# Feed-forward of a decoder layer: another order inside the slots, peaks taken tile by tile, a last tile that goes round GpSimd, and final scaling on VectorE

## What is computed

```
def _act_quant(x):
    scale = 127.0 / jnp.clip(jnp.max(jnp.abs(x), axis=-1, keepdims=True), 1e-05)
    return jnp.clip(jnp.round(x * scale), -128.0, 127.0) / scale
def _bitlinear(x, w):                       # _weight_quant: three values, one scale per matrix
    return einsum('bsi,oi->bso', _act_quant(x), _weight_quant(w))
x = _layernorm(x + xattn(x, ctx))
gate = silu(_bitlinear(x, w_gate))
up = _bitlinear(x, w_up)
x = _layernorm(x + _bitlinear(gate * up, w_down))
```

## Time and profile before

| what | us |
|---|---|
| median of three runs (lowest, highest) | 812.57 (811.95, 816.28) |
| the profiled execution, its own time | 812.0 |
| span of its trace | 809.3 |
| first product of the feed-forward (L1827) starts | 673.18 |
| last product (tile 31) starts | 789.78 |
| from there to the end of the span | 19.5 |
| busy: PE, DVE, ACT, POOL | 697.6, 638.6, 380.4, 376.9 |

### The profile page before, as it was taken

The page is one execution under the profiler, slowest core; times in us unless marked ns, Lnnn a source line. Parts: engine busy times, 40 slices in busy tenths (PEclk is TensorE's granted clock), DMA queues, the critical chain, the costliest instruction groups (busy, mean ns, idle before and its releaser), DMA issues. The chain is left out here.

```text
span 809.3 us, 12498 instructions
## 1 busy us (share of the span) xinstructions
PE 697.6 (86%) x4398; PEld 504.9 (62%) x4414; DVE 638.6 (79%) x1194; ACT 380.4 (47%) x697; POOL 376.9 (47%) x522
## 2 busy tenths in 40 slices
PE   3999998977998788997988998779999998888982
PEld 1388755855757666475775765457777774555552
DVE  2698778899778999798997882166888967899982
ACT  4432264201282401734015445555666666777773
POOL 0653424753147651456612811442551135586776
PEclk9999999989999999998999999969999999999998
DMA  8250056230052540443611474800000000000102
GB/s 294 87 95 11 0 119 141 53 43 10 1 104 53 163 46 1 78 78 116 59 47 52 130 151 146 302 1 2 2 2 2 2 2 2 1 27 27 54 27 79
DMA packets 37049, 52.79 MB, mean 65 GB/s; under 512 B 4761, under 2 KB 31386, under 8 KB 36732
## 3 DMA queue, kind: packets, MB, share of 16 engines
q0 software_dynamic: 7680, 16.77, 12.7%
q1 hardware_dynamic: 28604, 33.92, 12.7%
q10 hardware_dynamic: 704, 1.32, 0.6%
HBM read 31.04 MB, written 8.39 MB: 49 GB/s over the span
## 5 line engine op out<-in xcount | busy, mean ns | idle before, releaser
L644 ACT ACTIVATE yb<-banks 128x256 f32<-128x256 f32 x64 | 24.5, 386 | 229.1 <-PE banks L407 169.3
L398 PE MATMUL banks<-inv_m,spec_y 128*128 128x256 f32 x384 | 87.9, 381 | 8.8 <-POOL spec_y L765 8.8
L431 PE MATMUL banks<-xt_in,w_in 128*128 128x512 f32 x192 | 86.9, 609 | 2.9 <-DMA xt_in<-in_x_t 2.9
L398 PEld LDWEIGHTS banks<-inv_m,spec_y 128*128 128x128 f32 x384 | 72.2, 190 | 21.8 <-POOL spec_y L765 12.4
L764 POOL TENSOR_TENSOR spec_y<-prod 128x256 f32<-128x256 f32 x64 | 49.5, 773 | 63.3 <-DVE prod L989 62.2
L355 PE MATMUL banks<-z_cplx,fwd_m 128*128 128x256 f32 x240 | 71.8, 381 | 8.3 <-DVE prod L989 8.2
L356 PE MATMUL banks<-z_cplx,fwd_m 128*128 128x256 f32 x240 | 71.4, 379 | 0.0
L431 PEld LDWEIGHTS banks<-xt_in,w_in 128*128 128x128 f32 x192 | 37.2, 196 | 48.7 <-issue 48.5
L369 PE MATMUL banks<-z,fwd_m 128*128 128x256 f32 x168 | 46.8, 441 | 20.9 <-DVE sums_c L936 16.0
L369 PEld LDWEIGHTS banks<-z,fwd_m 128*128 128x128 f32 x168 | 37.0, 225 | 31.7 <-issue 20.4
L988 DVE TENSOR_TENSOR prod<-banks,spec_h 128x512 f32<-128x512 f32 x64 | 44.0, 687 | 15.1 <-POOL spec_y L765 7.5
(11 more groups left out here) (239 smaller groups left out, 1721.0 us busy)
## 6 DMA issues: line engine op xcount, KB each, us to landing
xt_in<-in_x_t SPq DMA_DIRECT2D x4, 1024.0 KB, 6.7
x_tok<-in_x SPq DMA_DIRECT2D x8, 512.0 KB, 4.3
x_tok<-in_b_out POOLq DMA_DIRECT2D x8, 512.0 KB, 12.4
x_scratch<-x_tok SPq DMA_DIRECT2D x8, 512.0 KB, 2.9
x<-x_scratch SPq DMA_DIRECT2D x8, 512.0 KB, 8.8
v_t<-left POOLq DMA_DIRECT2D x8, 511.5 KB, 5.5
x_t<-left POOLq DMA_DIRECT2D x8, 511.5 KB, 4.6
out<-x SPq DMA_DIRECT2D x7, 512.0 KB, 2.9
```

The costliest lines, as they stand in the source:

```text
L398: last = mm(bank[:, odd * 2 * P:(odd + 1) * 2 * P], spec_y[:, j + odd, part * D + h * P:part * D + (h + 1) * P], inv_m[:, o:o + 2 * P], st ...
L431: last = mm(proj_pair(b, t)[:, c * 512:(c + 1) * 512], w_in[:, k, TILES[t] * P:(TILES[t] + 1) * P], xt_in[:, k, c * 512:(c + 1) * 512], st ...
```

## The change

**Peaks of the input.** `x_peaks` (a chunk at once) becomes `x_peak_of` (one tile, 128x256 to 128x1). Chunks 0 to 4 are taken in the attention loop, one tile for each j from 12 to 31, at the end of the iteration; their floors and reciprocals follow at j = 15, 19, 23, 27, 31. Chunks 5 to 7 are taken in slots 0 to 11 of the feed-forward, one tile each, with the floors and reciprocals in slots 3, 7, 11. (Before: two chunks in the attention loop, six in the feed-forward.)

**Order in the slots.** TensorE: gate(s+1), turn_input(s+2), turn_hidden(s-2), up(s+1), down(s-3). ScalarE: evac_input ahead of evac_hidden. VectorE: add_down of tile s-4, not s-3. GpSimd: the four operations of chunk 7's norm go into slots 3 to 6.

**Last tile and tail.** VectorE rounds tile 31 (`round_last`); TensorE turns it into the two banks of the gate area (`turn_last`); ScalarE and VectorE each evacuate one half. Factors: tiles 24 to 27 together, then 28 and 29, then 30 and 31. GpSimd computes only these factors; VectorE does the eight 128x256 scalings (`scale_out`), in one step of add and multiply. Tiles 24 to 27 are stored in two transfers.

```diff
-X_LATE, X_EARLY = 22, 2
+X_LATE, X_EARLY = 12, 5
@@ tensor
                 if s == 0:
                     project(HALVES - 1)
+                if s + 2 in tiles:
+                    turn_input(s + 2)
+                if s - 2 == LAST:
+                    turn_last()
+                elif s - 2 in tiles:
+                    turn_hidden(s - 2)
+                if s + 1 in tiles:
+                    inner(s + 1, ps_up, w_up, h_ready, up_mm)
                 if s - 3 in tiles:
                     ...
                     down(s - 3)
-                if s - 2 in tiles:
-                    turn_hidden(s - 2)
-                if s + 2 in tiles:
-                    turn_input(s + 2)
-                if s + 1 in tiles:
-                    inner(s + 1, ps_up, w_up, h_ready, up_mm)
@@ scalar
+                if s + 2 in tiles:
+                    evac_input(s + 2)
                 if s - 2 in tiles:
                     evac_hidden(s - 2)
-                if s + 2 in tiles:
-                    evac_input(s + 2)
...
+            evac_hidden(LAST - 1)
+            square_out(LAST - 4)
+            evac_last()
+            for i in range(LAST - 3, TILES_ALL):
+                square_out(i)
@@ gpsimd
                 if s == 2:
-                    norm_chunk(CHUNKS - 1)
+                    norm_factors(CHUNKS - 1)
+                if s - 3 in range(CH):
+                    norm_tile(CHUNKS - 1, s - 3)
...
-            for k in range(CH):
-                out_factors(CHUNKS - 1 + k, CHUNKS - 1, k, k + 1)
-                normalize_out(CHUNKS - 1 + k, TILES_ALL - CH + k)
+            out_factors(CHUNKS - 2, CHUNKS - 2, 0, CH)
+            out_factors(CHUNKS - 1, CHUNKS - 1, 0, CH // 2)
+            out_factors(CHUNKS, CHUNKS - 1, CH // 2, CH, mean_first=True)
@@ vector
+                if c in range(X_EARLY):
+                    x_peak_of(c * CH + k)
+                    if k == CH - 1:
+                        x_scales(c)
...
+            hidden(LAST)
+            floor_peak(LAST)
+            hidden_scale(LAST)
+            round_last()
+            for i in range(LAST - 4, LAST - 2):
+                add_down(i)
+            evac_last()
+            for i in range(LAST - 2, TILES_ALL):
+                add_down(i)
+            for i in range(TAIL, TAIL + CH):
+                scale_out(CHUNKS - 2, i)
+            for i in range(TILES_ALL - CH, TILES_ALL):
+                scale_out(CHUNKS - 1 + i % CH // 2, i)
```

More of the change, by code:

```diff
@@ L1258, in attention_and_feed_forward @@
         tiles = range(TILES_ALL)
+        LAST = TILES_ALL - 1
+        TAIL = TILES_ALL - 2 * CH
+        ps_last = [ps_score[:, n * 512:(n + 1) * 512].bitcast(BF16)[:, 0:HALF] for n in range(2)]
         score_banks = ps_score[:].rearrange("p (r n) -> p r n", n=512)
@@ L1432, in turn_hidden, with turn_last @@
                 last.then_inc(ht_mm, 1)
+            def turn_last():
+                pe.wait_ge(last_rounded, 1)
+                for n in range(2):
+                    for t in range(FT // 2):
+                        o = n * HALF + t * P
+                        last = transpose(ps_last[n][:, t * P:(t + 1) * P], low_halves(hid[:, LAST % CH, o:o + P]), ident_b[:])
+                    last.then_inc(last_turned, 1)
             def down(i):
-                pe.wait_ge(ht_evac, i + 1)
+                if i < LAST:
+                    pe.wait_ge(ht_evac, i + 1)
                 if i >= 2:
@@ L1603, in _ @@
             squares(HALVES - 2)
-            for s in range(TILES_ALL + 4):
+            for s in range(TILES_ALL):
                 if s + 1 in tiles:
@@ L1868, in _ @@
                     normalize(i - 1)
-                c, late = divmod(j - X_LATE, CH)
-                if late == 0 and c in range(X_EARLY):
-                    x_peaks(c)
-                if late == 1 and c in range(X_EARLY):
-                    x_scales(c)
+                c, k = divmod(j - X_LATE, CH)
+                if c in range(X_EARLY):
+                    x_peak_of(c * CH + k)
+                    if k == CH - 1:
+                        x_scales(c)
             normalize(HALVES - 2)
```

99 lines of the change are left out of this document (64 added, 35 removed).

## The result

The changed kernel took 807.49 us (median of six runs, 806.41 to 808.48) where the kernel before took 813.34 beside it: ratio 0.9923, 95% interval 0.9907 to 0.9938, faster by 0.8%. The forecast was 808.0, with 808.5 as the border of faster.

A forecast was written before the change was run, and what follows sets the result against it. No engine was full; chains of waits set the pace, 3.74 us per feed-forward slot. Attention +3.6, feed-forward -2.0 and tail -6.2 gave -4.6: 807.4 from the profiled 812.0, forecast 808.0 given the 812.57 median, range 802.5 to 811.5.

The forecast's parts named there:

- Attention, +3.6: Attention loop: small reductions in odd j, with floors and reciprocals, delay VectorE's shift; two chunks go; 3.6 us slower.
- Rival E: Attention loop: reductions in odd j are hidden like the even ones; 804.4 us in all, chance 0.08.
- the cover in even j: Attention loop: VectorE's 0.58 us of idle time behind c_t, said to make the reduction there free.
- Feed-forward, slots 12 to 31, -3.1: Later feed-forward slots: four take 14.54 us instead of 14.9, 68.1 in all against 71.2.
- the ring: Feed-forward: new chain of waits through GpSimd's input rounding, 3.37 us per slot, 3.64 with factors every fourth slot.
- Rival B: Feed-forward: GpSimd's chain of waits doesn't hold, VectorE's 3.21 us is the slot; 800.9 us in all, chance 0.12.
- Rival C: Feed-forward: TensorE's 1.42 us wait returns per group, late factors making additions late; 817.9 us in all, chance 0.07.
- Slots 0 to 12, +1.1: Early feed-forward slots: small reductions, floors and reciprocals on VectorE make them 46.5 us instead of 45.4.
- The hold: VectorE's floors wait for GpSimd on a shared port: 0.8 us each in slots 3, 7, 11; tail 0.4.
- Rival D: Tail: VectorE's scalings and GpSimd's factors hold each other, half the gain; 811.1 us in all, chance 0.10.
- Tail, -6.2: Last product to end of span: 13.3 us instead of 19.5, with rounding and scalings on VectorE.
- the old ring: Feed-forward before the change: chain of waits through TensorE and ScalarE, 3.74 us per slot, which the new order cuts.

The follow-up runs named there:

- e1: Kernel before with only the tile-wise peaks added, old order and old tail: 815.73 us against 814.10, ratio 1.0016.
- e4: The changed kernel itself, run again on the chip of the experiments: 806.53 us, ratio 0.9914 to the kernel before.
- e7: Changed kernel with the peaks of chunks 0 to 4 each taken by one 128x1024 operation: 802.86 us against 813.09 for the kernel before.
- e8: Changed kernel with the attention loop's small reductions in even tiles only, two behind each c_t: 803.68 us against 813.09 for the kernel before.
- e9: Changed kernel with the old chunk-wise peaks put back, so new order and new tail alone: 802.82 us against 812.95 for the kernel before.
- e5: Changed kernel with TensorE's up matmuls ahead of both groups of transposes, hidden ones now first: 798.19 us against 813.09 for the kernel before.
- e6: Changed kernel with each 128x4 floor of four peaks split into four 128x1 operations: 806.31 us against 813.09 for the kernel before.
- e2: Kernel before with only the new order of the slots, old peaks and old tail: 810.71 us against 814.10, ratio 0.9966.

## Why the prediction was right, point by point

**Total.** 808.0 was forecast, 807.5 measured. The sum of changes was -4.6 and by the stretches -5.6; the base chosen (812.57) was 0.8 under the median that was then measured beside the changed kernel (813.34). The whole change was thus -5.85 and not -4.6, and the two errors nearly cancel, so the total is closer than its terms: that part is luck. The prediction also carried the 2.7 us around the span over unchanged; they became 1.8, a term that it put at nothing.

**Attention, +3.6: right (3.7, and 3.8 in e1 and e4),** with pairs of 8.67 and 9.06. Its reason, that the shift is queued behind the reduction and a delay at this place is passed on one to one, is shown by e7, e8 and e9. Rival E, which had the odd reductions hidden, is out. What was wrong is the size of the cover in even j, taken as 0.58 and really about 1.0; it didn't touch the sum.

**Feed-forward, slots 12 to 31, -3.1: right (-3.2),** step by step: 8.96 and 11.30 for 8.99 and 11.33. e5 is the proof of the ring. Rival B (VectorE's 3.21 as the slot) was wrong for this order and exact for e5's. Rival C did not come: the slot with the factors made no addition late.

**Slots 0 to 12, +1.1: wrong by 1.4, measured -0.25.** The term mis-sized is the 15.3 for slots 0 to 3, which took 14.03 (678.72 to 692.75). The prediction held slot 3's floor for 0.8, with the reserve that GpSimd may not have begun; it took 0.20 (692.34), and the rounding began at 692.50. The rest is the start of the loop, where 0.7 for TensorE was an estimate and the waits come to 0.3 (slot 1 took 3.47 for 3.14). Slots 4 to 11 took 31.10, forecast 31.2, with holds in slots 7 and 11 (0.90 each).

**The hold.** The Trainium skill, page SBUF — State Buffer, section Who interferes with whom, was right for the floors: 0.90 beside a rounding, 0.20 in slot 3 without one, and 0.34 for four narrow ones (e6). Without the rule the sum would have been 2.8 lower, not 2.4, since the tail's 0.4 rests on it too. Where it was applied to the tail (0.4 for holds between factors and scalings), the trace of after does not bear it out. The first three scalings take 1.05 us together, 0.32 from one to the next and 0.41 for the last, while GpSimd's `pow` of 128x2 runs from 799.96 to 800.77:

```profile
800.01 1.05 DVE L1951 TENSOR_SCALAR x<-x,mean_neg,f_rstd 128x256 f32<-128x256 f32 x3
```

Rival D, whose price rested on such holds, is out: the tail is 13.75, not 16. In none of the eleven traces with this tail does a scaling start later than its factors or the one ahead of it allow.

**Tail, -6.2: measured -5.8.** The chain is as written: rounding at 2.96 (forecast 2.95), down(29) at 4.26 (4.2), transposes at 5.13 (5.1), down(31) at 6.66 (6.9), its addition at 7.75 (7.9). Two terms were off. The scalings end at 11.06, forecast 10.75 (its own terms, 9.1 + 0.95 + 0.6, add to 10.65). The squares are done at 8.97 (9.1), but the factors for two tiles take 1.24 from there and not 0.95, 0.87 of it the `pow` of 128x2, and the last two scalings, which wait for it, end 0.85 later and not 0.6. And from there to the end it was 2.7, not 2.1: eight scalings come so close together that the transfers queue (five issues in 2.41 us, the last of them over 0.9 behind the last scaling), which the prediction had only in its bounds. The 0.4 for holds, of which VectorE shows none here, made up for part.

```profile
801.41 2.41 SPq L1286 DMA_DIRECT2D out<-x  x5
```

**What it did not see.** The tile-wise peaks and the order were costed as separate terms, and their product (1 us) fell into the feed-forward sum unnoticed because the ring was worked out for both together; only the traces of e1, e2 and e9 part them. And the prediction looked for what is late next behind the old ring, found GpSimd's rounding, and stopped there. It did not ask what stood behind the waiting instruction without needing it: the up matmuls, 7 to 8 us for one move of two lines.

## What to carry to other kernels

When an engine must wait at one instruction, look at what is queued behind it and does not need it: here putting the matmuls that the bound engine waits for ahead of the transposes that wait for a slow producer was worth more (7 to 8 us) than the whole change (5.6). A small operation added to a ring (a closed chain of waits, whose length is the distance from one round to the next) costs its full time or nothing, depending on which side of a wait it stands: 0.33 in odd tiles, 0 in even ones, so place it by the idle time behind it and measure that cover by filling it. Compare kernels by stretches counted from a common point inside the trace: here unchanged stretches agree within 0.5 us where the whole times of one kernel scatter by 2 to 7. Then check the sum against the medians: what the stretches leave out, here 0.7 to 0.9 us outside the span, shows only there.
